# First pass of a transformer layer kernel: K and V of four token tiles taken chunk by chunk as the weights land, the source in eight buffers, be2 added in place

## The reference

```python
src = _layernorm(x)
q, k, v = src @ Wq + bq, src @ Wk + bk, src @ Wv + bv
Q, K = elu(q) + 1, elu(k) + 1                    # 16 heads of 64
KV = einsum('bshd,bshm->bhdm', K, v)             # sum over all tokens
Z = 1 / (einsum('bshd,bhd->bsh', Q, K.sum(axis=1)) + EPS)
attn_out = einsum('bshd,bhdm,bsh->bshm', Q, KV, Z) @ Wo + bo
x1 = _layer_norm(src + attn_out, g1, be1)
y = gelu(x1 @ W1 + b1) @ W2 + b2
x = x + _layer_norm(x1 + y, g2, be2)
out = x + _layernorm(x) @ weight.T + pooled(_layernorm(x)) @ disha
```

## Time and profile before

| | |
|---|---|
| time, 3 runs | median 1597.16 us (1596.81 to 1598.06) |
| the profiled execution: its own time | 1596.18 us |
| its span, slowest core (core 4) | 1594.6 us (the eight: 1590.2 to 1594.6) |
| PE busy | 1513.3 us, 95% of the span |
| DVE / ACT / POOL busy | 959.7 / 542.6 / 501.4 us |
| mean granted TensorE clock, core 4 | 0.982 |

### The profile page before, as it was taken

The page is one execution under the profiler, slowest core; times in us unless marked ns, Lnnn a source line. Parts: engine busy times, 40 slices in busy tenths (PEclk is TensorE's granted clock), DMA queues, the critical chain, the costliest instruction groups (busy, mean ns, idle before and its releaser), DMA issues.

```text
span 1594.6 us, 27044 instructions; the slowest of 8 cores (1590.2 to 1594.6 us)
## 1 busy us (share of the span) xinstructions
PE 1513.3 (95%) x9428; PEld 902.9 (57%) x9428; DVE 959.7 (60%) x1042; ACT 542.6 (34%) x952; POOL 501.4 (31%) x438
## 2 busy tenths in 40 slices
PE   2699999999789999999999999999999999999995
PEld 1354545444356666666666666666666666666662
DVE  1466666665735675857657675765667576676314
ACT  1254554544543232332323233232323323232221
POOL 3564544445445223222222322222232322223101
PEclk9899999999889999999999999999999999999997
DMA  9877775566863122141212223121221322122111
GB/s 175 195 167 178 156 170 135 137 145 147 164 130 112 57 67 87 48 93 47 74 53 81 75 59 92 48 73 54 80 74 59 81 57 77 54 80 60 48 53 40
DMA packets 113428, 150.75 MB, mean 95 GB/s; under 512 B 67216, under 2 KB 75408, under 8 KB 113296
## 3 DMA queue, kind: packets, MB, share of 16 engines
q1 hardware_dynamic: 92656, 117.03, 24.8%
q0 software_dynamic: 14112, 25.70, 11.6%
q10 hardware_dynamic: 6528, 6.29, 1.7%
HBM read 117.53 MB, written 41.94 MB: 100 GB/s over the span
## 4 chain that ended last, share of the span: by engine, by line
PE 93%; issue 2%; DVE 1%; POOL 1%; ACT 1%; DMA 1%; DVEq 0%; ACTq 0%; SPq 0%; POOLq 0%
PE psH L1125 28%; PE psY L1103 28%; PE psY L445 14%; PE psS L692 7%; PE psS L494 7%; PE psS L416 6%; PE psH L424 1%; PE psS L437 1%; PE psY L416 1%; PE psS L582 1%; DMA arena<-x 1%; PE psY L494 0%; POOL arena L252 0%; DVE arena L341 0%; POOL arena L254 0%
## 5 line engine op out<-in xcount | busy, mean ns | idle before, releaser
L1125 PE MATMUL psH<-arena 128*128 128x256 bf16 x4096 | 531.6, 273 | 1.4 <-ACT arena L572 1.4
L1103 PE MATMUL psY<-arena 128*128 128x512 bf16 x2048 | 525.8, 379 | 1.6 <-ACT arena L1031 1.2
L1031 ACT ACTIVATE arena<-psH,arena 128x256 bf16<-128x256 f32 x512 | 242.4, 474 | 765.1 <-PE psH L1125 763.3
L1125 PEld LDWEIGHTS psH<-arena 128*128 128x128 bf16 x4096 | 401.0, 98 | 144.9 <-issue 1.6
L1103 PEld LDWEIGHTS psY<-arena 128*128 128x128 bf16 x2048 | 200.3, 98 | 135.1 <-issue 3.0
L445 PE MATMUL psY<-arena 128*128 128x512 bf16 x1024 | 236.2, 386 | 15.8 <-DMA arena<-Wk 9.5
L603 DVE RECIPROCAL arena<-arena 128x512 f32<-128x512 f32 x56 | 187.3, 3345 | 52.4 <-ACT arena L593 52.4
L445 PEld LDWEIGHTS psY<-arena 128*128 128x128 bf16 x1024 | 100.0, 99 | 134.3 <-issue 24.7
L543 POOL TENSOR_TENSOR arena<-arena 128x1024 f32<-128x1024 f32 x32 | 69.0, 2157 | 237.3 <-ACT arena L539 229.2
L489 POOL TENSOR_TENSOR arena<-arena 128x1024 f32<-128x1024 f32 x32 | 69.3, 2166 | 216.9 <-ACT arena L484 213.5
L503 DVE TENSOR_TENSOR arena<-psS,arena 128x512 f32<-128x512 f32 x60 | 41.3, 689 | 149.1 <-PE psS L494 148.9
(11 more groups left out here) (113 smaller groups left out, 1338.1 us busy)
## 6 DMA issues: line engine op xcount, KB each, us to landing
arena<-x SPq DMA_DIRECT2D x64, 512.0 KB, 4.9
xb_s<-arena SPq DMA_DIRECT2D x32, 512.0 KB, 5.0
arena<-W POOLq DMA_DIRECT2D x64, 256.0 KB, 7.1
arena<-xb_s SPq DMA_DIRECT2D x32, 512.0 KB, 3.2
out<-arena SPq DMA_DIRECT2D x32, 512.0 KB, 2.9
arena<-qt_s SPq DMA_DIRECT2D x16, 512.0 KB, 3.3
qt_s<-arena ACTq DMA_DIRECT2D x24, 256.0 KB, 7.1
arena<-WfT SPq DMA_DIRECT2D x16, 256.0 KB, 2.9
```

Of the source, the lines that this page charges most:

```text
L1031: sc.activation(hT[n % 3][:, :], hbank[n % 2], AF.Gelu, bias=b1c[:, c:c + 1]).then_inc(b_g, 1)
L1103: ii = te.matmul(ybank[k], hT[n % 3][:, (k // 2) * P:(k // 2 + 1) * P], w2_v[c][:, (k % 2) * HALF:(k % 2 + 1) * HALF], start=(c == 0), sto ...
L1125: ii = te.matmul(hbank[n % 2], w1_v[c // NCH][:, w, (c % NCH) * P:(c % NCH + 1) * P], x1T[i % 2][:, w, :], start=(w == 0), stop=(w == NCH ...
```

## The change

PE starts K and V of tiles 0 to 3 on the chunks of the weights as they land. Each chunk of Wk and of Wv has a semaphore of its own. K of tiles 0, 1 and 2 is interleaved, chunk by chunk, in three pairs of PSUM banks (psK, psV and psH, which `kv_sum` doesn't use yet), K of tile 3 follows in psK, then V of tiles 0 and 1 is interleaved as Wv lands, in psV and psH. V of tiles 2 and 3, the first sums of KV, and K and V of tile 4 follow, and then the first two pieces of Q stand back to back. From tile 5 on the order is that of before.

For that the source has more buffers in the first half of the pass. Tiles 0 to 15 go round eight: `xbuf` and six more in the room that the last chunks of W2 take later. `x_be2` of these tiles adds be2 in place, and the store to memory goes out of the same buffer, with a semaphore for each (`s_xo`), so that the load of tile t + 8 waits for the store of tile t. From tile 16 on the two buffers and `xbst` of before are used. POOL does no `x_be2` before its iteration 4; a table XB spreads them over the iterations up to 15. Tiles 0 to 3 have more room for K as well (`k_buf`, `z_buf`, `e_buf`).

```diff
+            x_load(0)
             sy.dma_start(identb[:, :], idb_d).then_inc(s_id, 16)
+            for t in range(1, 4):
+                x_load(t)
+            for dst, src in [(bqc, bqc_d), (bk1b, bkb_d)]:
+                sy.dma_start(dst[:, :], src).then_inc(s_const, 16)
+            sy.wait_ge(s_wk[NCH - 1], 16)
+            x_load(4)
+            x_load(5)
+            sy.wait_ge(s_wv[NCH - 1], 16)
+            x_load(6)
+            for dst, src in [(be2b, be2_d), (onesb, one_d), (b1c, b1_d), (bvc, bvc_d)]:
+                sy.dma_start(dst[:, :], src).then_inc(s_rows, 16)
+            x_load(7)
             for t in range(T):
...
+                x_keep(t)
+                if t < 10:
+                    x_load(t + 8)
+                elif 16 <= t < T - 2:
+                    x_load(t + 2)
...
+        XB = {4: [0], 5: [1, 2], 6: [3], 7: [4, 5], 8: [6], 9: [7, 8], 10: [9], 11: [10, 11],
+              12: [12], 13: [13, 14], 14: [15, 16], 15: [17]}
...
-            x_be2(0)
-            x_be2(1)
-            for t in range(T):
-                if t + 2 < T:
-                    x_be2(t + 2)
-                k_sum(t)
...
+            gp.wait_ge(a_src, 6)
+            for t in range(4):
+                k_sum(t)
+                w_load(t)
+            for t in range(4, T):
+                for u in (XB[t] if t < 16 else [t + 2] if t + 2 < T else []):
+                    x_be2(u)
+                k_sum(t)
+                w_load(t)
...
+                if t == 4:
+                    q_exp(sc, 0)
+                    rstd(6)
+                if t < T - 4:
                     q_exp(sc, 2 * (t - 4) + 1)
...
             src_tr(0)
-            for t in range(T):
+            src_tr(1)
+            for w in range(NCH):
+                if w == 0:
+                    te.wait_ge(a_ev, 1)
+                te.wait_ge(s_wk[w], 16)
+                part(0, w, k_bank(0), wk_v, a_k)
+                if w == 1:
+                    te.wait_ge(a_ev, 2)
+                    part(1, 0, k_bank(1), wk_v, a_k)
+                if w >= 1:
+                    part(1, w, k_bank(1), wk_v, a_k)
+                if w == 3:
+                    src_tr(2)
+                if w == 5:
+                    te.wait_ge(a_ev, 3)
+                    for u in range(5):
+                        part(2, u, k_bank(2), wk_v, a_k)
+                if w >= 5:
+                    part(2, w, k_bank(2), wk_v, a_k)
+                if w == 6:
+                    src_tr(3)
+            te.wait_ge(a_ev, 4)
+            te.wait_ge(a_z, 1)
+            proj(3, k_bank(3), wk_v, a_k)
+            te.wait_ge(a_z, 3)
+            for w in range(NCH):
+                te.wait_ge(s_wv[w], 16)
+                part(0, w, v_bank(0), wv_v, a_v)
+                part(1, w, v_bank(1), wv_v, a_v)
+            src_tr(4)
...
+            te.wait_ge(s_wq, 16 * NCH)
+            q_proj(te, 0)
+            q_proj(te, 1)
+            for t in range(5, T):
```

More of the change, by code:

```diff
@@ L98, in build_nc @@
         ebf = VB(W + 51200, D)
+        xe = [VF(2048 * (16 + 2 * k), D) for k in range(6)]
+        kx = [VB(2048 * 28, D), VB(2048 * 29, D)]
+        zf1, ebf1 = VF(2048 * 14, D), VB(2048 * 30, D)
         slot = [VF(W + 4096 * k, D) for k in range(6)]
@@ L317, in act_a @@
             evac(0)
-            for t in range(T):
-                if t + 1 < T:
+            rstd(2)
+            evac(1)
+            rstd(3)
+            evac(2)
+            evac(3)
+            for t in range(4):
+                k_exp(t)
+            rstd(4)
+            v_out(0)
+            v_out(1)
+            evac(4)
+            rstd(5)
+            v_out(2)
+            v_out(3)
+            evac(5)
+            sc.wait_ge(a_mem, 6)
+            for t in range(4, T):
+                if 5 <= t < T - 1:
                     evac(t + 1)
-                if t + 2 < T:
+                if 5 <= t < T - 2:
                     rstd(t + 2)
@@ L384, in dve_a @@
             stats(0)
+            norm(0)
             stats(1)
-            norm(0)
             norm(1)
+            stats(2)
+            stats(3)
+            norm(2)
             v.wait_ge(s_const, 32)
@@ L390, in dve_a @@
             v.tensor_scalar(bq1c[:, :], bqc[:, :], 1.0, None, ALU.add).then_inc(a_mem, 1)
-            stats(2)
-            for t in range(T):
-                if t + 2 < T:
+            norm(3)
+            k_in(0)
+            k_in(1)
+            k_out(0)
+            k_in(2)
+            k_out(1)
+            k_in(3)
+            stats(4)
+            norm(4)
+            k_out(2)
+            k_out(3)
+            stats(5)
+            norm(5)
+            for t in range(4, T):
+                if 5 <= t < T - 2:
                     norm(t + 2)
@@ L396, in dve_a @@
                 k_out(t)
-                if 4 <= t < T - 4:
+                if t == 4:
+                    stats(6)
+                    norm(6)
+                if t < T - 4:
                     q_out(v, 2 * (t - 4))
@@ L449, in proj, with part @@
                 ii.then_inc(done, 1)
-            src_tr(0)
-            for t in range(T):
+            def part(t, w, ps, wgt, done):
+                for nh in range(2):
+                    ii = te.matmul(ps[:, nh * 512:(nh + 1) * 512],
+                                   srcT[0][:, w, t * P:(t + 1) * P],
+                                   wgt[:, w, nh * 512:(nh + 1) * 512],
+                                   start=(w == 0), stop=(w == NCH - 1))
+                if w == NCH - 1:
+                    ii.then_inc(done, 1)
+            src_tr(0)
+            src_tr(1)
+            for w in range(NCH):
+                if w == 0:
[21 more added lines that the diff above has]
+            te.wait_ge(a_z, 3)
+            for w in range(NCH):
+                te.wait_ge(s_wv[w], 16)
+                part(0, w, v_bank(0), wv_v, a_v)
+                part(1, w, v_bank(1), wv_v, a_v)
+            src_tr(4)
+            te.wait_ge(a_z, 4)
+            proj(2, v_bank(2), wv_v, a_v)
+            te.wait_ge(a_vb, 2)
+            kv_sum(te, 0)
+            proj(3, v_bank(3), wv_v, a_v)
+            kv_sum(te, 1)
+            src_tr(5)
+            te.wait_ge(a_ev, 5)
+            te.wait_ge(a_vb, 3)
+            proj(4, psK, wk_v, a_k)
+            kv_sum(te, 2)
+            te.wait_ge(a_vb, 4)
+            proj(4, psV, wv_v, a_v)
+            kv_sum(te, 3)
+            te.wait_ge(s_wq, 16 * NCH)
+            q_proj(te, 0)
+            q_proj(te, 1)
+            for t in range(5, T):
                 if t + 1 < T:
```

146 lines of the change are left out of this document (84 added, 62 removed).

## The result

The changed kernel takes 1586.42 us (median of 4 runs, 1585.66 to 1586.66) against 1597.13: ratio 0.993, 95% interval 0.9914 to 0.9945. It is faster by 10.7 us. Forecast were 26.7 us and 1570.5, with a range from 1564 to 1581, so the direction was right and the time lies outside the range.

A forecast was written before the change was run, and what follows sets the result against it. Transfers were taken to bound the pass up to 58 us, PE after. First piece of Q at 62.7 against 90.8, less 1.4 for the pair, gave 26.7 us: median 1597.16 becomes 1570.5, range 1564 to 1581.

The forecast's parts named there:

- What bounds the kernel: Whole pass: bound by transfers up to 58 us and by PE behind that, without waits from 58.05 on.
- the first part of the sum: Start of the pass: Wk lands at 27.8, Wv at 44.2, Wq at 62.7, where the first piece of Q starts.
- p = 2.0 us: Start of the pass: cost of each 512 KB transfer from SP beside POOL's weight loads, bounds 1.4 and 2.9 us.
- The pair of Q: Two first pieces of Q, back to back in one bank: the second waits 1.4 us for ACT's reading.
- the rival of a low clock while the chunks trickle in: PE from Wk's end: half clock puts the first piece of Q at 69.5, gain 19.9 us, 1577.3; chance 0.12.
- the one on ACT and DVE: Around the first pieces of Q: added ACT and DVE work is hidden, except 1.4 us for the pair's reading.
- the one behind it on POOL: POOL and SP after Wq: tile 8 in at 78 with 8.5 us to spare; POOL takes 7 of 11.25 us a tile.
- 90.8: Kernel before: time in us at which the same work is done as at the changed kernel's first piece of Q.
- The rival of a starved tile 8: Tiles 8 to 12: slower transfers bring tile 8 11.5 us later, PE stands 3 or 10; 1573.5 to 1580; chance 0.10.
- 5.4 for a store: SP's queue: the store behind x_be2(0) takes 5.4 us, then the load of tile 8 takes 6.1.
- What POOL's issues wait for: POOL's weight loads: at most 14 chunks outstanding, so w_load(3)'s issue waits until Wq is in; x_be2(0) at about 64.
- the order of the sum: Whole pass: 90.8 - 62.7 - 1.4 = 26.7 us gained, with the same PE work in the same order behind.

The follow-up runs named there:

- the second experiment: Changed kernel plus one wait: in iterations 4 to 15 POOL starts its be2 additions only after DVE's norm of tile t + 2; 1570.84 us, ratio 0.9829.
- the versions with waits: Changed kernel with POOL waiting for DVE's norm in iterations 4 to 15: the second experiment (1570.84 us) and the latter version (1569.12 and 1569.28 us).
- the latter version: As the second experiment, with be2's addition to tile 0 one iteration earlier and no pair of additions before iteration 7; 1569.12 and 1569.28 us, ratio 0.9829.
- the third experiment: Changed kernel with the deviation of tile 6 ahead of the first piece of Q on ACT, no other edit; 1585.87 us, ratio 0.9924.
- the last experiment: Kernel before the change with one semaphore for each chunk of Wk and Wv, no other edit; 1593.17 us, ratio 0.9973.

## Why the prediction was wrong

*What bounds the kernel, and the first part of the sum:* right. The weights landed 0.5 to 2 us before the times that p = 2.0 us gave (Wv 43.67 for 44.2; Wq, for which core 4 waited until 60.69, for 62.7), and the first piece of Q began at 61.02 in place of 62.7. It was PE, not Wq, that came last on the slowest core; on core 4 PE waited 0.5 us for Wq.

*The pair of Q:* right, 1.51 us for 1.4.

*The clock:* the rival of a low clock while the chunks trickle in didn't happen. From 26 to 60 us the granted clock was 1.00 in each of the stretches read, with PE busy for 5.3 of 6 us and 7.2 of 8; its two waits for chunks in that time were 0.89 and 1.25 us. The clock did cost something where nothing was forecast: after the 6.9 us of idle time it was 0.58 in the mean from 73 to 80 us.

*The step that failed* is the one on ACT and DVE and the one behind it on POOL: "`norm(6)` on DVE and the transposes of tile 6 on PE wait for it; that ends at about the time of the second piece and costs nothing more", and "POOL has ... 7 of 11.25 us". I counted POOL's additions as load on POOL and asked only whether it keeps up. It does. What they cost DVE I left out, though the page before had a sign of it: `q_out` of 0.68 us took 2.97 at times. DVE and POOL of the kernel before, core 4:

```profile
95.26 2.97 DVE L341 SCALAR_TENSOR_TENSOR arena<-arena 128x512 bf16<-128x512 bf16 x1 [1.51 <-ACT arena L278]
```

```profile
95.28 2.38 POOL L240 TENSOR_TENSOR arena<-arena 128x1024 f32<-128x1024 f32 x1
```

Two additions back to back where one had stood, and three in 10 us behind the held issue, made the hold longer: 8.21 us for a norm and 5.47 for a `q_out`. In us on PE, worked out on core 7: 6.9 idle, 2.8 at the lower clock (73.23 to 79.88 in place of 3.9), 9.8 - 1.5 = 8.3 for ACT's readings. From the 90.8 - 61.0 = 29.8 won at the first piece of Q, 1.5, 6.9, 2.8 and 8.3 are lost again. That leaves 10.3; the spans of the slowest cores differ by 9.8, and the medians by 10.7.

*The rival of a starved tile 8* had the right place, POOL's held issue, and the wrong cause, transfers. A part of it is true: the chain from the first addition over the store to tile 8 is longer than the medians of the earlier trace rows said. In the changed kernel, 8.5 us lie between SP's issue of the store and that of the load behind it, where I took 5.4 for a store:

```profile
64.73 0.33 SPq L272 DMA_DIRECT2D xb_s<-arena  x1
73.21 0.33 SPq L265 DMA_DIRECT2D arena<-x  x1
```

In the second experiment, with the norm no longer in the way, DVE waited 3.14 us for tile 8.

*What POOL's issues wait for* was wrong as well. I read the gaps at 26 and 38 us as a limit of 14 chunks that is freed eight at a time. With a semaphore for each chunk they are freed one by one (the 15th issued at 10.37, the 16th at 13.97), and only the 31st, behind Wq with its shared semaphore, waited until Wq was in. It changed the sum little, since Wq was as late in the queue anyway.

With PE no longer waiting for a held DVE, the versions with waits come to 1570.84 and 1569.2 us against the 1570.5 forecast, so the order of the sum was right. That they hit it so closely is partly luck. In the latter version the last pair of projections of the pass begins at 349.80 (core 2), before at 376.46 (core 4): 26.7 us earlier, the number of the prediction. But the first piece of Q began there at 60.48, 2.2 us before the forecast, and about 2 us were lost behind it that the sum didn't have: 0.9 for the norm of tile 6, 0.6 for a second reading of Q, and some tenths each time PE starts again.

## What to carry to other kernels

When work is moved or bunched on POOL, look at what DVE does at that time. Count every DVE instruction that takes two operands from SBUF, and every fast `tensor_scalar`, as possibly as long as POOL's run without a pause, and see who waits for it. If PE does, let POOL wait for a DVE event, or at least for the end of its own instruction; a wait can be worth 1% of the kernel. And an engine's share of busy time says nothing about this: POOL was busy for 31% of the span, before and after.

## What the runs showed of the hardware that was not expected

A DVE instruction can be held through several POOL instructions in a row, 10.53 us for one of 0.80, if they follow without a gap, and is let in by a gap of 0.27 us. Between an addition and the `k_sum` behind it without a wait, the second starts 0.06 us before the first has ended by the profile (62.30 + 2.36 against 64.60). The `q_out` of 5.47 us even began 0.25 us before the pair that held it, during POOL's DMA issue (123.26 and 123.51).

In the changed kernel the two DMA issues behind `k_sum(4)`, 1.1 us, let the norm in on two cores and not on six. The norm had begun 0.06 to 0.37 us after `k_sum(4)` on the six cores where it stayed out, and 0.72 and 0.77 us after it on those where it got in (3, 0); the second experiment lets it in there too, at 0.72 (67.89 and 68.61). But the distance alone doesn't explain the third experiment, where the norm began 1.1 to 1.5 us into the first addition on four cores and stayed out, and got in on core 7 at 0.94. The three cores on which it got in have something else in common: POOL's first addition stood 0.14 to 0.46 us behind the DMA issue before it (on two of them the bracket names the load of bvc), while on the other thirteen cores of the two kernels it followed at once. Which of these decides wasn't tried, and why the hold outlasts one POOL instruction stays open.

POOL's limit of chunks outstanding is released by their semaphores: chunks that share one are released together, at the last. That it is so is shown by the issue times in both kernels and in the last experiment; how it is done isn't.
